# Cross-attention on one core: copied rows of reciprocals, transfers over all partitions, and another order on ACT and in the first unit

## The chip, the cores and the metric

The kernel runs on one core of one Trainium2 chip. The metric is the device time of one execution in microseconds (us). The kernel before was run three times: 1737.68, 1738.79 and 1740.34 us, median 1738.79 us.

## The reference

Sixteen batches of 1024 queries (x, 512 wide) attend to 64 context rows each, with 16 heads of 64. The residual is added, and the sum goes through a layer norm:

```
qh = x @ Wq + bq;  kh = ctx @ Wk + bk;  vh = ctx @ Wv + bv
attn = exp(qh.kh * mask - max(over everything)) * mask
attn = attn / (sum over keys + 1e-15)
y = (attn @ vh) @ Wo + bo + x
out = (y - mean) / sqrt(var + 1e-5) * gamma + beta
```

The maximum is one number over all batches and heads, so no exponential can be taken before every score is known.

## The kernel before

The program has two phases. **scores_phase** (to about 905 us of the span) computes all masked scores. Heads go in pairs: a tile has 128 partitions (two heads of 64 keys) and 512 queries, and a unit is 8 such pairs for 512 queries. There are 32 units. The scores of units 0 and 1 stay in SBUF (`s32`), those of the other 30 go to DRAM. The products of the value weights and Wo (`u`) go to DRAM too.

**output_phase** is where the diff lies. Its loops run over 8 groups of 4 units. For each unit:

- SP loads the scores (2 MB, `load_scores`), the residual x (1 MB, `load_x`), for every second unit u (2 MB, `load_u`), and stores y (1 MB, `store_y`, L774), which waits until POOL has finished the unit.
- ACT takes the exponentials of the scores in place in two halves of 1.9 us (`exps`, L884). `tiny` (L892) fills the bank of sums first.
- PE sums them over the keys of each head with 16 small matmuls (`sums`, L832), into 32 rows of each of four quarters. DVE inverts the sums (`invert`, L966).
- SP writes the reciprocals to DRAM (`store_r`, L743: 4 transfers of 8 rows) and reads them back over the partitions (`spread_r`, L751: 4 transfers, each one 8 KB row to 64 partitions, 512 KB), since each of the 64 key rows of a head needs the same reciprocals. Between them SP waits for the stores to land (L754).
- DVE multiplies the exponentials by the reciprocals (`scale_p`, L973), ACT rounds the product to f16 (`round_p`, L898), DVE takes the rest (`split_p`, L983). Eight pairs, three PSUM banks in turn.
- PE multiplies both halves by u for four tiles of 128 queries (`unit`, L846: 96 matmuls), and behind the fourth pair of the third tile come the sums of the unit three further on. Four output banks, which ACT fills with the bias beforehand (`fill`, L904).
- DVE adds the residual and takes mean and variance (`residual`, L988: L997, L1000, L1002), POOL makes 1/std and the shift (`inv_std`, L1063), ACT normalizes (`norm`, L909), POOL multiplies by gamma and adds beta (`affine`, L1076: L1080, L1082).

Every engine takes its instructions in a fixed order written out by hand. Within the turn of unit n PE multiplies unit n, DVE and ACT make the halves of unit n+1 (p 0 to 7), ACT takes the exponentials and PE the sums of unit n+3. DVE's order (L1004) is: scale 0, 1, split 0, scale 2, split 1, residual 0, scale 3, split 2, scale 4, split 3, residual 1, scale 5, split 4, scale 6, split 5, scale 7, split 6, invert, residual 2, split 7, residual 3. ACT's order before (L914) is halves 0 and 1, tiny, first half of the exponentials, halves 2 and 3, fill 0, norm 0, second half, halves 4 and 5, fill 1, norm 1, halves 6 and 7, fill 2, norm 2, fill 3, norm 3. POOL alternates `inv_std` and `affine` for the tiles 0 to 3. SP's order (L796) is store_y of the last unit, load_scores of the unit four on, load_x, load_u, store_r and spread_r of the unit three on.

At the start of the phase SP issues loads of scores 2 and 3, u, the three rows gamma, beta and bo over 128 partitions, and x 0 and 1. PE's first five matmuls, which only write the banks once, wait for u (L870), and ACT's first instruction waits for them (L941).

Of the kernel before, what the change touches and what calls it, by code (L numbers as in the profile page):

```python
# [5 lines left out]
F32 = mybir.dt.float32  # L6
# [26 lines left out]
SBANKS, GBANKS, OBANKS, RBANKS = 2, 4, 4, 3  # L33
EARLY = NP // 2
# [8 lines left out]
def build(nc, xT, x, ctxT, maskT, wk, wqT, wv, wo, bk, bq, bv, bo, gamma, beta,  # L43
# [4 lines left out]
    r_d = nc.dram_tensor("reciprocals", (UNITS, 2, NP, TT), F32, kind="Internal").ap()  # L48
# [621 lines left out]
def output_phase(nc, x, scores_d, u_d, r_d, bo, gamma, beta, sel_sum_d, out,  # L670
# [4 lines left out]
    with ExitStack() as ctx:  # L675
# [59 lines left out]
        def _(sp):  # L735
# [7 lines left out]
            def store_r(n, u):  # L743

                sp.wait_ge(r_done, n + 1)
                for q in range(4):
                    th, a = q // 2, q % 2
                    sp.dma_start(r_d[u % UNITS, :, 4 * a:4 * a + 4, th * HT:(th + 1) * HT],
                                 r32[32 * q:32 * q + NP, u % 2, :]).then_inc(r_stored, 16)

            def spread_r(n, u):  # L751


                sp.wait_ge(r_stored, 64 * n + 64)  # L754
# [29 lines left out]
            load_scores(3, 3)  # L784
# [44 lines left out]
        def _(pe):  # L829
# [44 lines left out]
            pe.wait_ge(sum_in, 16)  # L874
# [7 lines left out]
        def _(act):  # L882
# [31 lines left out]
            def group(g, last):  # L914
                for u in range(UNITS):
                    n, s = g * UNITS + u, (u + 1) % 2
                    more, more3 = not (last and u == UNITS - 1), not (last and u >= UNITS - 3)
                    halves = lambda *ps: [round_p(n + 1, s, p) for p in ps] if more else None
                    halves(0, 1)
                    if more3:  # L920
                        tiny(n + 3)
                        exps(n + 3, u + 3, 0)
                    halves(2, 3)
                    if more:
                        fill(n + 1, 0)
                    norm(g, u, 0)
# [12 lines left out]
                    norm(g, u, 3)  # L939
# [10 lines left out]
            for t in range(TB):  # L950
                fill(0, t)
# [5 lines left out]
            with act.Fori(0, NG - 1) as g:  # L957
                group(g, False)
            group(NG - 1, True)

        @block.vector
        def _(dve):
# [3 lines left out]
            def invert(n, u):  # L966

                dve.wait_ge(e_summed, n + 1)
                if not (isinstance(n, int) and n < 2):
                    dve.wait_ge(r_stored, 64 * (n - 1))  # L970
                dve.reciprocal(r32[:, u % 2, :], ps_sum[:, 0:HT]).then_inc(r_done, 1)  # L971

            def scale_p(n, u, p):  # L973
                s = u % 2
                if p % 4 == 0:
                    dve.wait_ge(bc_in[s][p // 4], 16 * n - 16 * s + 32)
# [159 lines left out]
```

## Time and profile before

| | before |
|---|---|
| median of three runs | 1738.79 us |
| the profiled execution | 1738.39 us |
| its span | 1736.5 us |
| mean granted TensorE clock | 0.982 |
| PE, DVE, ACT, POOL busy | 93%, 66%, 54%, 31% |
| output phase, from / to | about 905 / 1736.5 us |

The busy shares are means over both phases. POOL works only in the second, so its 544.1 us are two thirds of that phase. Times below are counted from the start of the span. A row of the timeline gives start, length, engine, line, what is written and read, count, and in brackets how long the engine had been idle and what ended that.

### The profile page before, as it was taken

The page shows a single profiled execution, that of the slowest core. Times are in us where ns is not written, and L with a number is a line of the kernel's source. Part 1 is how long each engine was busy: PE and PEld are TensorE (multiplying, and loading weights), DVE is VectorE, ACT ScalarE, POOL GpSimd, SP SyncE. Part 2 cuts the span into 40 slices and gives each one's busy share as a digit, 9 for nine tenths or more (in the row PEclk, how much of TensorE's full clock was granted, in tenths as well). Part 3 has the DMA queues.
Part 4 walks back from the last instruction along what each step waited for, and adds up shares of the span by engine and source line. Part 5 has one row for each costly group of instructions (what it writes and reads, how often), then busy time and mean ns, then how long its engine had stood idle before and what let it go on. Part 6 is the DMA issues. An engine that isn't in the chain of part 4 may idle for free. (4 is left out here: it accounts for less than half of the span.)

```text
span 1736.5 us, 30465 instructions
## 1 busy us (share of the span) xinstructions
PE 1619.3 (93%) x10501; PEld 796.7 (46%) x10501; DVE 1151.8 (66%) x2138; ACT 935.5 (54%) x1383; POOL 544.1 (31%) x778
## 2 busy tenths in 40 slices
PE   4999999999999999999983999999999999999997
PEld 4445555455554555545531344444444444444443
DVE  6666555565556655566542777878778787878774
ACT  6755555555555555555534555555555555555542
POOL 0000000000000000000000567677666767677677
PEclk8999999999999999999995999999999999999999
DMA  6463444534445444453327999999999999999971
GB/s 231 146 226 121 164 176 151 222 122 160 172 157 217 127 154 172 163 211 128 153 97 247 265 308 314 290 286 292 313 318 295 291 313 316 278 293 297 310 234 73
DMA packets 92556, 382.11 MB, mean 220 GB/s; under 512 B 7520, under 2 KB 12768, under 8 KB 74592
## 3 DMA queue, kind: packets, MB, share of 16 engines
q1 hardware_dynamic: 92512, 381.53, 65.7%
q8 instruction: 27, 0.44, 0.1%
q14 instruction: 17, 0.14, 0.0%
HBM read 250.43 MB, written 131.07 MB: 220 GB/s over the span
## 5 line engine op out<-in xcount | busy, mean ns | idle before, releaser
L78 PE MATMUL ps_o<-u,p_hi 128*128 128x512 f16 x1024 | 389.7, 381 | 5.0 <-DVE p_lo L985 5.0
L69 PE MATMUL ps_s<-x_hi,g_hi 128*128 128x512 f16 x1024 | 389.1, 380 | 3.7 <-ACT s L496 3.7
L79 PE MATMUL ps_o<-u,p_hi 128*128 128x512 f16 x1024 | 389.4, 380 | 0.0
L80 PE MATMUL ps_o<-u,p_lo 128*128 128x512 f16 x1024 | 389.2, 380 | 0.0
L71 PE MATMUL ps_s<-x_hi,g_lo 128*128 128x512 f16 x1024 | 388.8, 380 | 0.0
L70 PE MATMUL ps_s<-x_lo,g_hi 128*128 128x512 f16 x1024 | 388.6, 380 | 0.0
L496 ACT ACTIVATE s<-ps_s,c_bias 128x512 f32<-128x512 f32 x256 | 176.1, 688 | 314.1 <-PE ps_s L71 311.0
L1052 POOL MEMSET zeros<- 128x256 f32 x1 | 0.3, 311 | 905.9 <-POOLq L138 905.9
L985 DVE TENSOR_TENSOR p_lo<-ps_p,p_hi 128x512 f16<-128x512 f32 x256 | 175.4, 685 | 126.3 <-ACT p_hi L902 126.0
L616 DVE TENSOR_TENSOR score_max<-score_max,tile_max 128x1 f32<-128x1 f32 x257 | 40.7, 158 | 310.5 <-ACT s L496 308.8
L912 ACT ACTIVATE y<-y,shift,rstd 128x512 f32<-128x512 f32 x128 | 104.1, 813 | 243.4 <-POOL shift L1073 238.9
L1080 POOL TENSOR_TENSOR y<-y,gamma_b 128x512 f32<-128x512 f32 x128 | 163.4, 1277 | 118.4 <-ACT y L912 118.4
L1082 POOL TENSOR_TENSOR y<-y,beta_b 128x512 f32<-128x512 f32 x128 | 191.9, 1499 | 10.0
L626 DVE CUSTOM_DVE_ANT_0 s<-s,mask_add 128x512 f32<-128x512 f32 x256 | 176.4, 689 | 0.3 <-issue 0.3
L902 ACT ACTIVATE p_hi<-ps_p 128x512 f16<-128x512 f32 x256 | 140.7, 584 | 49.7 <-DVE ps_p L980 49.7
L78 PEld LDWEIGHTS ps_o<-u,p_hi 128*128 128x128 f16 x1024 | 100.3, 98 | 138.5 <-issue 12.8
L69 PEld LDWEIGHTS ps_s<-x_hi,g_hi 128*128 128x128 f16 x1024 | 100.2, 98 | 127.1 <-issue 10.8
L80 PEld LDWEIGHTS ps_o<-u,p_lo 128*128 128x128 f16 x1024 | 100.5, 98 | 121.6 <-issue 1.5
L71 PEld LDWEIGHTS ps_s<-x_hi,g_lo 128*128 128x128 f16 x1024 | 100.3, 98 | 121.3 <-issue 0.8
L79 PEld LDWEIGHTS ps_o<-u,p_hi 128*128 128x128 f16 x1024 | 100.5, 98 | 116.8 <-issue 0.6
L70 PEld LDWEIGHTS ps_s<-x_lo,g_hi 128*128 128x128 f16 x1024 | 100.3, 98 | 112.8 <-issue 0.8
L980 DVE TENSOR_TENSOR ps_p<-s_more,r_bc 128x512 f32<-128x512 f32 x128 | 116.5, 921 | 5.4 <-DMA r_bc<-reciprocals 4.1
(90 smaller groups left out, 2363.1 us busy)
## 6 DMA issues: line engine op xcount, KB each, us to landing
r_bc<-reciprocals SPq DMA_DIRECT2D x128, 512.0 KB, 8.1
scores<-s SPq DMA_DIRECT2D x30, 2048.0 KB, 7.6
x<-xT_in SPq DMA_DIRECT2D x32, 1024.0 KB, 9.5
u_halves<-u_out SPq DMA_DIRECT2D x64, 512.0 KB, 3.2
s_more<-scores SPq DMA_DIRECT2D x16, 2048.0 KB, 16.3
u<-u_halves SPq DMA_DIRECT2D x16, 2048.0 KB, 22.3
y<-x_in SPq DMA_DIRECT2D x32, 1024.0 KB, 18.1
out<-y SPq DMA_DIRECT2D x31, 1024.0 KB, 12.3
```

The costliest lines, as they stand in the source:

```text
L69: pe.matmul(out, lhs_hi, rhs_hi, start=first, stop=False)
L70: pe.matmul(out, lhs_hi, rhs_lo, start=False, stop=False)
L71: return pe.matmul(out, lhs_lo, rhs_hi, start=False, stop=last)
L78: pe.matmul(out, lhs_hi, rhs_hi, start=False, stop=False, skip_group_check=True)
L79: pe.matmul(out, lhs_hi, rhs_lo, start=False, stop=False, skip_group_check=True)
L80: return pe.matmul(out, lhs_lo, rhs_hi, start=False, stop=False, skip_group_check=True)
L496: act.activation(s32[:, u % 2, p, :], ps_s[p % SBANKS][:, :], ACT.Identity, bias=c_bias[:, k:k + 1], scale=1 / (G_SCALE * X_SCALE)).then_i ...
L626: dve.tensor_tensor_reduce(s32[:, u % 2, p, :], s32[:, u % 2, p, :], mask_add[:, j, t0:t0 + TT], 1.0, MASKED, ALU.add, ALU.max, tile_max[: ...
L902: act.activation(p_hi[:, s, p, :], ps_p[p % RBANKS][:, :], ACT.Copy).then_inc(p_hi_done, 1)
L985: dve.tensor_tensor(p_lo[:, s, p, :], ps_p[p % RBANKS][:, :], p_hi[:, s, p, :], ALU.subtract)\
L1080: pool.tensor_tensor(y, y, gamma_b[:, :], ALU.mult).then_inc(scaled, 1)
L1082: pool.tensor_tensor(y, y, beta_b[:, :], ALU.add).then_inc(shifted, 1)
```

## The change

It has four parts.

1. **Copies.** The selection matrix gives each sum not once but four times, in 16 rows per head (16 h + p + 4 j); the matmuls keep their shape. `store_r` writes these rows twice, so that DRAM holds eight copies: 16 transfers of 16 rows of 1 KB (256 KB) instead of 4 of 8 rows. `spread_r` is 2 transfers instead of 4, each over all 128 partitions (1 MB); 16 source rows of 8 KB (2 heads x 8 copies), each read by 8 partitions.
2. **ACT's order.** In a unit: tiny, half 0, fill 3 of this unit, half 1, exponentials' first half, norm 2 of the unit before, half 2, exponentials' second half, half 3, norm 3 of the unit before, fill 0, halves 4 and 5, norm 0, fill 1, halves 6 and 7, norm 1, fill 2. Norms 2 and 3 are thus taken in the next unit's turn. The first group is taken out of the loop.
3. **Start of the phase on SP.** Scores 3 and x 1 are loaded only behind the first store_r and spread_r.
4. **First matmuls.** The five matmuls that write the banks take the selection matrix (64 KB) and scores already in SBUF (f32) instead of u, and wait for that load alone.

```diff
-    r_d = nc.dram_tensor("reciprocals", (UNITS, 2, NP, TT), F32, kind="Internal").ap()
+    r_d = nc.dram_tensor("reciprocals", (UNITS, 2, 2, COPIES, NP // 2, TT), F32, kind="Internal").ap()
...
                 for q in range(4):
                     th, a = q // 2, q % 2
-                    sp.dma_start(r_d[u % UNITS, :, 4 * a:4 * a + 4, th * HT:(th + 1) * HT],
-                                 r32[32 * q:32 * q + NP, u % 2, :]).then_inc(r_stored, 16)
+                    for c in range(0, COPIES, 4):
+                        for h in range(2):
+                            rows = 32 * q + 16 * h
+                            sp.dma_start(r_d[u % UNITS, a, h, c:c + 4, :, th * HT:(th + 1) * HT]
+                                         .rearrange("c p t -> (c p) t"),
+                                         r32[rows:rows + 16, u % 2, :]).then_inc(r_stored, 16)
...
                 for k in range(2):
-                    for h in range(2):
-                        rows = r_d[u % UNITS, h:h + 1, 4 * k:4 * k + 4, :].rearrange("a p t -> a (p t)")
-                        sp.dma_start(r_bc[rows_of(h), u % 2, 4 * k:4 * k + 4, :].rearrange("r p t -> r (p t)"),
-                                     rows.to_broadcast([NK, 4 * TT])).then_inc(bc_in[u % 2][k], 16)
+                    rows = r_d[u % UNITS, k, :, :, :, :].rearrange("h c p t -> (h c) (p t)").unsqueeze(1)
+                    sp.dma_start(r_bc[:, u % 2, 4 * k:4 * k + 4, :].rearrange("r p t -> r (p t)"),
+                                 rows.to_broadcast([2 * COPIES, P // (2 * COPIES), 4 * TT])).then_inc(bc_in[u % 2][k], 16)
...
             load_scores(2, 2)
-            load_scores(3, 3)
             load_u(0, B - 1)
...
             load_x(0, 0)
+            store_r(0, 0)
+            spread_r(0, 0)
+            load_scores(3, 3)
             load_x(0, 1)
-            for n in range(2):
-                store_r(n, n)
-                spread_r(n, n)
+            store_r(1, 1)
+            spread_r(1, 1)
             store_r(2, 2)
...
-            pe.wait_ge(u_in[0], 16)
-            for o in (*ps_o, ps_sum):
-                mm = pe.matmul(o[:, :], u2[:, 0, 0, 0, 0:P], u2[:, 0, 0, 0, :], start=True, stop=True)
+            pe.wait_ge(sum_in, 16)
+            for o in (ps_sum, *ps_o):
+                mm = pe.matmul(o[:, :], sel_sum[:, :, :].rearrange("r a b -> r (a b)"), scores_of(0)[:, 0, :],
+                               start=True, stop=True)
...
-                    halves(0, 1)
+                    behind = lambda t: None if first and u == 0 else norm(g if u else g - 1, (u - 1) % UNITS, t)
                     if more3:
                         tiny(n + 3)
+                    halves(0)
+                    fill(n, 3)
+                    halves(1)
+                    if more3:
                         exps(n + 3, u + 3, 0)
-                    halves(2, 3)
+                    behind(2)
+                    halves(2)
+                    if more3:
+                        exps(n + 3, u + 3, 1)
+                    halves(3)
+                    behind(3)
                     if more:
                         fill(n + 1, 0)
+                    halves(4, 5)
                     norm(g, u, 0)
-                    if more3:
-                        exps(n + 3, u + 3, 1)
-                    halves(4, 5)
                     if more:
                         fill(n + 1, 1)
+                    halves(6, 7)
                     norm(g, u, 1)
-                    halves(6, 7)
                     if more:
                         fill(n + 1, 2)
-                    norm(g, u, 2)
-                    if more:
-                        fill(n + 1, 3)
-                    norm(g, u, 3)
...
-            sel_sum[h * NK:(h + 1) * NK, p % 4, 4 * h + p % 4] = 1.0 / P_SCALE
+            sel_sum[h * NK:(h + 1) * NK, p % 4, 16 * h + p % 4:16 * h + 16:4] = 1.0 / P_SCALE
```

## Rows read from the trace of the kernel before

**Rows 1.** The page: shares of the engines in the chain that ended last.

```profile
POOL 21%; DVE 10%; issue 6%; ACT 5%; DMA 3%; SPq 1%; DVEq 1%; ACTq 0%; PE 0%; POOLq 0%
```

**Rows 2.** Waits from 1200 to 1400: total us, times, longest.

```profile
ACT y L912 <- POOL shift L1073: 62.4, 25, 4.1
...
PE ps_sum L841 <- ACT s_more L890: 5.9, 4, 1.5
```

**Rows 3.** Timeline of PE, the sums of units 2, 3 and 28.

```profile
1017.71 2.11 PE L841 MATMUL ps_sum<-s,sel_sum 128*32 128x256 f32 x32
1040.58 1.07 PE L841 MATMUL ps_sum<-s_more,sel_sum 128*32 128x256 f32 x16
...
1649.84 1.07 PE L841 MATMUL ps_sum<-s_more,sel_sum 128*32 128x256 f32 x16
1652.77 1.07 PE L841 MATMUL ps_sum<-s_more,sel_sum 128*32 128x256 f32 x16 [1.86 <-ACT s_more L890]
```

**Rows 4.** Timelines of POOL, DVE and ACT within one unit.

```profile
1321.57 1.27 POOL L1080 TENSOR_TENSOR y<-y,gamma_b 128x512 f32<-128x512 f32 x1 [0.93 <-ACT y L912]
1322.91 1.60 POOL L1082 TENSOR_TENSOR y<-y,beta_b 128x512 f32<-128x512 f32 x1
...
1321.88 3.19 DVE L980 TENSOR_TENSOR ps_p<-s,r_bc 128x512 f32<-128x512 f32 x2
...
1326.05 0.81 ACT L912 ACTIVATE y<-y,shift,rstd 128x512 f32<-128x512 f32 x1 [4.08 <-POOL shift L1073]
```

**Rows 5.** Groups of the output phase by form: busy us, mean ns, idle before.

```profile
L985 DVE TENSOR_TENSOR p_lo<-ps_p,p_hi 128x512 f16<-128x512 f32 x256 | 175.4, 685 | 126.3 <-ACT p_hi L902 126.0
...
L902 ACT ACTIVATE p_hi<-ps_p 128x512 f16<-128x512 f32 x256 | 140.7, 584 | 49.7 <-DVE ps_p L980 49.7
...
L1000 DVE BATCH_NORM_STATS2 stats<-y 128x6 f32<-128x512 f32 x128 | 88.9, 694 | 4.4
L997 DVE SCALAR_TENSOR_TENSOR y<-ps_o,y 128x512 f32<-128x512 f32 x128 | 85.8, 670 | 15.0 <-PE ps_o L80 12.4
...
L971 DVE RECIPROCAL r<-ps_sum 128x256 f32<-128x256 f32 x32 | 56.0, 1749 | 28.2 <-PE ps_sum L841 28.2
```

**Rows 6.** Stretches: length, busy us (count) of PE, PEld, DVE, ACT, POOL, clock, DMA share, GB/s.

```profile
910.00:922.00 12.00, 0.00 (x0) 0.00 (x0) 0.15 (x1) 0.00 (x0) 0.48 (x4) 0.50 1.01 430
925.00:927.00 2.00, 2.00 (x5) 0.46 (x3) 0.00 (x0) 0.00 (x0) 0.00 (x0) 0.50 1.01 194
...
942.00:948.00 6.00, 3.74 (x32) 1.28 (x32) 1.40 (x1) 2.54 (x2) 0.00 (x0) 0.58 1.01 218
```

**Rows 7.** Start of the output phase: timelines of PE, ACT, DVE and SP.

```profile
924.74 1.89 PE L872 MATMUL ps_o<-u 128*128 128x512 f16 x4 [20.45 <-DMA u<-u_halves]
...
927.50 7.66 ACT L890 ACTIVATE s<-s,neg_max 128x2048 f32<-128x2048 f32 x4
...
914.77 0.15 DVE L1038 TENSOR_SCALAR neg_max<-key_max 128x1 f32<-128x1 f32 x1 [7.89 <-POOL key_max L1055]
...
948.27 1.27 DVE L980 TENSOR_TENSOR ps_p<-s,r_bc 128x512 f32<-128x512 f32 x2
...
935.23 2.62 SPq L748 DMA_DIRECT2D reciprocals<-r  x4
939.02 2.41 SPq L760 DMA_DIRECT2D r_bc<-reciprocals  x4
```

**Rows 8.** Issues of spreads (ns min/median/max), and of loads (KB, us to landing).

```profile
L760 SPq DMA_DIRECT2D r_bc<-reciprocals x128: 496/592/1382, 939.0 to 1670.6; - x128
...
s_more<-scores SPq DMA_DIRECT2D x16, 2048.0 KB, 16.3
```

**Rows 9.** Last unit: timelines of POOL and DVE.

```profile
1706.39 0.19 POOL L1066 TENSOR_TENSOR var_eps<-mean_var,ln_eps 128x1 f32<-128x1 f32 x1 [0.17 <-DVE mean_var L1002]
...
1732.70 1.26 POOL L1082 TENSOR_TENSOR y<-y,beta_b 128x512 f32<-128x512 f32 x1
...
1723.98 0.69 DVE L997 SCALAR_TENSOR_TENSOR y<-ps_o,y 128x512 f32<-128x512 f32 x1 [3.51 <-PE ps_o L80]
```

More of the change, by code:

```diff
@@ L33 @@
 SBANKS, GBANKS, OBANKS, RBANKS = 2, 4, 4, 3
+COPIES = 8
+STORES_R = 2 * COPIES
 EARLY = NP // 2
@@ L747, in store_r @@
                     th, a = q // 2, q % 2
-                    sp.dma_start(r_d[u % UNITS, :, 4 * a:4 * a + 4, th * HT:(th + 1) * HT],
-                                 r32[32 * q:32 * q + NP, u % 2, :]).then_inc(r_stored, 16)
+                    for c in range(0, COPIES, 4):
[4 more added lines that the diff above has]
+                                         r32[rows:rows + 16, u % 2, :]).then_inc(r_stored, 16)
             def spread_r(n, u):
-                sp.wait_ge(r_stored, 64 * n + 64)
+                sp.wait_ge(r_stored, 16 * STORES_R * (n + 1))
                 if isinstance(n, int) and n == 2:
@@ L867, in group @@
                     unit(g, u, last)
-            pe.wait_ge(u_in[0], 16)
-            for o in (*ps_o, ps_sum):
-                mm = pe.matmul(o[:, :], u2[:, 0, 0, 0, 0:P], u2[:, 0, 0, 0, :], start=True, stop=True)
+            pe.wait_ge(sum_in, 16)
+            for o in (ps_sum, *ps_o):
+                mm = pe.matmul(o[:, :], sel_sum[:, :, :].rearrange("r a b -> r (a b)"), scores_of(0)[:, 0, :],
+                               start=True, stop=True)
             mm.then_inc(o_written, 1)
-            pe.wait_ge(sum_in, 16)
             for n in range(3):
@@ L912, in norm, with group @@
                 act.activation(y, y, ACT.Identity, bias=shift[:, t:t + 1], scale=rstd[:, t:t + 1]).then_inc(normed, 1)
-            def group(g, last):
+            def group(g, first, last):
                 for u in range(UNITS):
@@ L918, in group @@
                     halves = lambda *ps: [round_p(n + 1, s, p) for p in ps] if more else None
-                    halves(0, 1)
+                    behind = lambda t: None if first and u == 0 else norm(g if u else g - 1, (u - 1) % UNITS, t)
                     if more3:
                         tiny(n + 3)
+                    halves(0)
+                    fill(n, 3)
+                    halves(1)
+                    if more3:
                         exps(n + 3, u + 3, 0)
-                    halves(2, 3)
+                    behind(2)
[4 more added lines that the diff above has]
+                    behind(3)
                     if more:
                         fill(n + 1, 0)
+                    halves(4, 5)
                     norm(g, u, 0)
-                    if more3:
-                        exps(n + 3, u + 3, 1)
-                    halves(4, 5)
                     if more:
                         fill(n + 1, 1)
+                    halves(6, 7)
                     norm(g, u, 1)
-                    halves(6, 7)
                     if more:
                         fill(n + 1, 2)
-                    norm(g, u, 2)
-                    if more:
-                        fill(n + 1, 3)
-                    norm(g, u, 3)
+                if last:
+                    norm(g, UNITS - 1, 2)
+                    norm(g, UNITS - 1, 3)
             act.wait_ge(o_written, 1)
@@ L949, in _ @@
             act.wait_ge(affine_in, 48)
-            for t in range(TB):
+            for t in range(TB - 1):
                 fill(0, t)
@@ L956, in _ @@
                 round_p(0, 0, p)
-            with act.Fori(0, NG - 1) as g:
-                group(g, False)
-            group(NG - 1, True)
+            group(0, True, False)
+            with act.Fori(1, NG - 1) as g:
+                group(g, False, False)
+            group(NG - 1, False, True)
         @block.vector
@@ L969, in invert @@
                 if not (isinstance(n, int) and n < 2):
-                    dve.wait_ge(r_stored, 64 * (n - 1))
+                    dve.wait_ge(r_stored, 16 * STORES_R * (n - 1))
                 dve.reciprocal(r32[:, u % 2, :], ps_sum[:, 0:HT]).then_inc(r_done, 1)
@@ L975, in scale_p @@
                 if p % 4 == 0:
-                    dve.wait_ge(bc_in[s][p // 4], 16 * n - 16 * s + 32)
+                    dve.wait_ge(bc_in[s][p // 4], 8 * n - 8 * s + 16)
                 if p >= RBANKS or not (isinstance(n, int) and n == 0):
```

## The prediction

> **What bounds the kernel now.** I read the page first. PE is the busiest engine by far, yet the chain that ended last has POOL with 21%, DVE with 10% and PE with 0% [rows 1]. So somewhere PE waits for a ring of the others. The waits of a stretch in the middle say where: in each unit PE waits 1.5 us for the exponentials (5.9 us in four waits on one buffer, and the same again on the other), while ACT itself has waited up to 4.1 us for POOL's shift [rows 2]. The exponentials are late because they stand in ACT's order behind norms and halves that wait.
>
> What this costs is read from the starts of the sums. Unit 3 has them at 1040.58 and unit 28 at 1649.84, so 25 periods of 24.37 us. Unit 2 has both halves of its sums in one piece of 2.11 us and is followed by unit 3 after 22.87 us [rows 3]. So 22.87 us is a unit in which PE doesn't wait, and 24.37 us one with its wait of 1.5. PE can give at most 1.50 us per unit.
>
> The start of the phase is bound otherwise. PE waits 20.45 us for u, and only then can the first exponential begin, at 927.50, although the negated maximum is there at 914.77 + 0.15 [rows 7].
>
> **Start of the phase.** The selection matrix is 64 KB and the first transfer that the phase issues; I estimate its landing at 908.5, some 3 us into the phase, as the 8 KB stores need 3.8 us from the first of four issues to all landed [rows 7]. Five f32 matmuls with 512 columns follow. The nearest row is the pair of sum blocks of unit 2: 32 records, 2.11 us, four groups of 256 columns one after the other, 0.53 each [rows 3], so 1.06 for 512 columns at 2.4 GHz and 2.1 at 1.2 GHz. The granted clock was 0.50 from 910 on, after PE had stood still [rows 6]. Both ends: 908.5 + 5.3 = 914, and 908.5 + 10.5 = 919. I take 917.5, since PE begins again before the level fell. With the filling of the sums' bank the exponentials start at 918 instead of 927.5: 9.5 us earlier (12 at most).
>
> From there to the first scaling it was 20.8 us (948.27 - 927.50), and DVE got there through three inversions. Now the stores are 16 instead of 4. Four took 2.62 us, 0.64 each, and the first spread was issued 3.8 us after the first store [rows 7]. Sixteen take 10.2 and land 1.2 later. First reciprocals at 918 + 7.7 = 925.7, landed at 937, first spread (1 MB) at 430 GB/s 2.5 us plus 1.5: scaling starts at 941, gain 7.3 us. The longer chain of stores eats 2 of the 9.5.
>
> Unit 1's reciprocals then stand behind 3 MB of loads (7.4 us) and 16 more stores, so that they are there at about 955, where the sums of unit 3 are due at 959: PE waits some 1.5 us. Unit 2's come behind 5 MB (12.5 us), at about 979, and cost PE about 1.5 more. Before, these two units cost more: from the first scaling at 948.27 to the start of unit 2 (its sums at 1017.71, less 20 of the 32 steps of a unit's 22.87 - 2.11 = 20.76 us ahead of them, so 1004.7) were 56.4 us. Mine are 941 to 995. **Start: 9.7 us.**
>
> **The transfers.** While only spreads were in flight the DMA moved 218 GB/s at full share, and 430 while it was loads [rows 6]. A unit's 2.1 MB of reciprocals so take 9.7 us, and its 5.2 MB of loads and stores 12.2; that is 22 of 24.4 us. Which property of the spreads costs the half? Two are candidates: 64 partitions per transfer, and one source row read by all. The gamma, beta and bo loads read one row too, go to all partitions, and moved 194 GB/s [rows 6]. The new transfer changes both: 128 partitions, and 16 rows. I take 430 GB/s, thus 4.9 us, and keep 9.7 as the other end.
>
> The Trainium skill's page "SBUF — State Buffer" (The DMA port swizzle) says that a transfer to partitions 0 to 63 reaches eight of sixteen ports, about 218 GB/s, and one to all partitions up to 436. By it alone the copies would be needless; the load of one row at 194 GB/s speaks against its being the whole story, and both readings give 4.9 us here.
>
> Stores: 16 issues at 0.64 are 10.2 us of SP's time instead of 2.6; spreads 2 at 0.6 are 1.2 instead of 2.4. SP's turn grows by 6.4 us per unit. The bounds for one are the shortest and the longest issue of a spread, 0.5 and 1.38 [rows 8]; I take 0.64, from the stores themselves.
>
> **ACT's order: the new ring.** Start from norm 0. Lengths are those of [rows 4, 5, 7], less 0.1 where two follow on one engine (four exponentials took 7.66, so 1.9 each); a fill is taken as long as a half, both being one ACT pass over 128x512. Norm 0, fill 1, half 6: 0.7 + 0.5 + 0.6 = 1.8. DVE: split 6 0.6, inversion 1.7, residual 2 1.6 (0.67 + 0.69 and the aggregate), split 7 0.6, residual 3 1.6, scale 0 0.7 = 6.8. ACT: half 0 0.5, fill 3 0.5, half 1 0.5, exponentials 1.9 = 3.4. Then norm 2 to POOL 0.9, affine 2 1.27 + 1.60 = 2.9, inv_std 3 1.55 (from 1324.51 to norm 3 at 1326.05), norm 3 0.9, affine 3 2.9, inv_std 0 1.7 = 10.9. **The ring is 22.9 to 23.0 us**, just at PE's 22.87. Inside it the second half of the exponentials ends 3.1 us after norm 2 starts, ahead of PE's need, so the wait of 1.5 goes. What is late next is DVE's scale 0: it is behind residual 3, and that behind everything.
>
> Cover that thins: norm 2 now waits for the exponentials, so store_y, and load_scores behind it on SP, come some 4 us later in a unit, and the scores are wanted some 5 us earlier. From affine 3's end to the next use are 11.5 us; the landing took 16.3 in the middle [rows 8]. But that queue held 9.7 us of spreads. In order: stores end, land, spread issued, 4.9 us of spreads, 1 MB out and 2 MB scores 7.4 us, 1.5 to land. With SP's stores from the inversion on (15 us after norm 2), and a period P, the load lands at 15.05 - P + 10.2 + 1.9 + 4.9 + 7.4 + 1.5 = 41 - P after norm 2, and must be there at P - 1.9: satisfied for P above 21.4. No wait at 23.0, with 3 us to spare. PE's instructions, the number and size of the matmuls of the sums, POOL's and DVE's work are the same.
>
> 25 periods x (24.37 - 23.0) = 34.3 us, and unit 28, whose period had 0.4 us more wait (1.86), 1.8.
>
> **The end.** POOL's last run goes from 1706.39 to 1733.96 without a pause, while PE ends at 1723.9 [rows 9]. By the new order POOL enters the last three units up to 5.7 us later, and there PE's unit (20.8 us, no sums) is no longer than POOL's round (four times 0.9 + 2.9 + 1.55, so 21.4), so this isn't caught up: I count 5 us lost, between 0 and 5.7.
>
> **Sum:** 9.7 + 34.3 + 1.8 - 5.0 = 40.8 us of the profiled execution's 1738.39, so 1697.6; against the median of 1738.79, 0.4 above it, 1698.0. The scores phase is untouched.
>
> **Rivals.**
>
> *The ring is longer* (22%). Scale 0 falls beside POOL's affine 1. Two scales beside affine 2 took 3.19 us [rows 4], two undisturbed 1.27 [rows 7]. One such delay of 0.8 in the ring gives P = 23.8: 25 x 0.57 = 14 us, so 1718; half of it 1708. For: it is a matter of a few tenths. Against: affine 1 is nearly over by then. The page "SBUF — State Buffer" calls the port pair that DVE and GpSimd share an exclusive lock, held for a whole instruction; by it scale 0 would wait for the whole of a 1.27 or 1.60 us instruction, and the sum would be the 1718 of this case.
>
> *Spreads stay at 218 GB/s* (7%): 9.7 in place of 4.9 gives 2P = 45.8 + 1.9, P = 23.9; the start gains 4 less. About 1724.
>
> *Only the start gains* (5%): something else holds the period at 24.37 and the end loses its 5: 1734.
>
> *SP becomes the bound* (8%): this one is slower. SP waits in turn for stores, spreads, then store_y and the scores. With i us per store the formula is 2P = 32.7 + 16 i; at 0.64 P = 21.5 doesn't bind, it equals the old 24.37 at i = 1.0, and the whole is slower than before from 1.05 on, since the longer stores eat the start's gain too and the end loses its 5. At 1.38 P is 27.4 and the time 1738.8 + 25 x 3.0 = about 1814; at 1.1, 25.1 and 1757. For: stores with 16 rows are a form not yet seen, behind a full queue. Against: the four took 2.62, and the new ones are as short.
>
> *The change doesn't do it at all* (3%): the five f32 matmuls or the fetch of a first group outside the loop eat the start, the ring stays: within 0.2%.
>
> **How the numbers follow.** My forecast has 55%, with its own range 1686 to 1706 (P from 22.87 to 23.2, start 7 to 12, end 0 to 5.7). With the longer ring it reaches 1720, and with slow spreads 1727. 1686 to 1727 holds some 82%. A difference under 0.2% (3.5 us) can't be told from none here. Faster by more: 55 + 22 + 7 + 5 = 89, less a little for their tails, 88%; same 4%; slower 8%.
>
> **What would show it.** Right: PE's waits on L890 vanish from the middle and the sums of two units lie 22.9 to 23.1 apart; stretches with spreads alone show above 400 GB/s; the first exponential starts between 915 and 919; 16 stores take about 10 us; POOL never waits for DVE's mean but for ACT's norm 2. Wrong: PE still waits there; ACT's exponentials wait for s or s_more from the DMA; SP's queue shows store_y or load_scores waiting behind the stores; scale 0 at 1.5 us each time.

## The result, and the profile after

The changed kernel is slower: 1829.43 us, median of four runs (1828.32 to 1832.28), against 1738.66 for the kernel before (1737.68 to 1740.34). The ratio is 1.0523, 95% interval 1.0505 to 1.0542. The forecast was 1698.

I take the loss apart by the starts of the sums, as in [rows 3]. PE of the changed kernel:

```profile
1042.17 2.08 PE L848 MATMUL ps_sum<-s_more,sel_sum 128*32 128x256 f32 x32
...
1735.13 1.93 PE L848 MATMUL ps_sum<-s_more,sel_sum 128*32 128x256 f32 x16 [5.05 <-ACT s_more L897]
```

Unit 3 has its sums at 1042.17 and unit 28 at 1735.13. The period is therefore 27.72 us where it was 24.37. That is 25 x 3.35 = 83.7 us. The start is 1.6 later than before, and from unit 28's sums to the end of the span it is 91.0 instead of 86.7, so 4.3 more. Together 89.6, the difference of the spans (1826.1 and 1736.5). The mean granted clock fell from 0.982 to 0.951 along with PE's waits; in e8 and e15 below, where PE hardly waits, it is 0.985. ("Unit 3" and "unit 28" are here, as in [rows 3], the turns in which PE multiplies these units; the sums in them belong to the unit three further on.)

The page's chain that ended last, engines and then lines (before: [rows 1]):

```profile
DMA 24%; POOL 9%; SPq 6%; ACT 4%; issue 4%; DVE 2%; PE 0%; ACTq 0%; DVEq 0%; POOLq 0%
DMA reciprocals<-r 8%; DMA s<-scores 7%; DMA s_more<-scores 7%; SPq L753 5%; POOL y L1096 3%; POOL y L1094 3%; ACT y L919 2%; DVE r L985 1%; POOL rstd L1084 1%; DMA r_bc<-reciprocals 1%; SPq L766 1%; POOL var_eps L1080 1%; POOL shift L1087 1%; ACT p_hi L909 1%; ACT s L897 1%
```

POOL and DVE led it before with 31% together; now DMA and SP's queue have 30%, most of it by the landings of the stores (8%) and of the scores (7% and 7%). The waits from 1200 to 1400 (total, times, longest; before: [rows 2]), of the engines:

```profile
POOL y L1094 <- ACT y L919: 73.3, 28, 11.3
...
ACT s L897 <- DMA s<-scores: 20.3, 4, 7.3
...
PE ps_sum L848 <- ACT s L897: 13.5, 6, 4.6
ACT s_more L897 <- DMA s_more<-scores: 11.2, 3, 7.0
```

And of SP in the same stretch:

```profile
SPq L766 <- DMA reciprocals<-r: 78.3, 7, 12.1
SPq L753 <- DVE r L985: 22.8, 7, 3.5
SPq L783 <- POOL y L1096: 11.0, 3, 4.1
```

PE waits for the exponentials, they wait up to 7.3 us for the scores' landing, and SP stands 11 us per unit in the wait for the stores. Its timeline has the whole ring:

```profile
1306.33 7.32 SPq L753 DMA_DIRECT2D reciprocals<-r  x16
1325.62 1.20 SPq L766 DMA_DIRECT2D r_bc<-reciprocals  x2
1327.09 0.41 SPq L783 DMA_DIRECT2D out<-y  x1
1327.76 0.37 SPq L741 DMA_DIRECT2D s<-scores  x1
1328.32 0.38 SPq L773 DMA_DIRECT2D y<-x_in  x1
1331.97 8.03 SPq L753 DMA_DIRECT2D reciprocals<-r  x16
1350.64 1.19 SPq L766 DMA_DIRECT2D r_bc<-reciprocals  x2
...
1362.02 7.35 SPq L753 DMA_DIRECT2D reciprocals<-r  x16
```

Sixteen stores are issued from 1306.33 to 1313.65 and seen landed at 1325.62, 12.0 us after the last. Only then go out the spreads and the scores' load (1327.76). Those scores land at 1345.31, when ACT begins their exponentials after 7.29 us of idling; their stores begin at 1362.02. The round from store to store is 55.7 us for two units, or 27.8 for one. The granted clock falls behind PE's wait, to 0.50 from 1349 to 1353. This doesn't visibly lengthen the round: from the waited-for exponentials to the next stores it is 16.7 us here and 16.7 in e1 below (1349.43 to 1366.14), where the clock was 0.78 or more in each stretch of 4 us. Meanwhile the queue (length, busy us of the engines, clock, DMA share, GB/s; before: [rows 6]):

```profile
1300.00:1306.00 6.00, 6.00 (x29) 2.72 (x28) 4.08 (x5) 2.30 (x4) 4.87 (x10) 1.00 1.01 218
1306.00:1312.00 6.00, 6.00 (x29) 2.74 (x28) 5.70 (x11) 2.91 (x6) 4.84 (x8) 1.00 1.04 391
...
1323.50:1327.00 3.50, 3.50 (x18) 1.57 (x17) 3.50 (x5) 0.98 (x2) 3.42 (x5) 1.00 0.02 7
```

The spreads still move 218 GB/s, as before. The bulk loads follow, the stores land only behind them, and then for 3.5 us hardly anything is in flight (share 0.02), until the next spread begins.

The same ring was there in the kernel before, where it did not bind yet. Its timeline of SP:

```profile
1317.96 2.55 SPq L748 DMA_DIRECT2D reciprocals<-r  x4
1330.27 2.41 SPq L760 DMA_DIRECT2D r_bc<-reciprocals  x4
```

And its waits of SP from 1200 to 1400:

```profile
SPq L760 <- DMA reciprocals<-r: 68.6, 8, 9.9
```

Four stores took 12.3 us from their first issue to the next spread; sixteen now 19.3. With 9.7 of spreads, 12.2 of bulk and about 2.2 idle, I estimate that the old queue needed 24.1 of the 24.37 us. The estimate is a little low: where this ring binds with the same stores and spreads (e1 and e3 below), the period is 24.56 and 24.66. That it didn't bind before is seen in the starts of the sums, which lie 24.36 to 24.38 us apart in every unit from 3 to 28. In e1 they lie 22.69 to 26.55 apart, and in the changed kernel up to 29.4.

### The profile page after: what moved, and what is told of

Same layout as the page of the kernel before. It is cut to its first block and busy times, and to the rows that moved or that the text cites. A ratio compares the mean times of both kernels' runs of the same rounds, so it can differ in the third digit from the quotient of the medians.

```text
span 1826.1 us, 30718 instructions
## 1 busy us (share of the span) xinstructions
PE 1667.3 (91%) x10506; PEld 807.6 (44%) x10506; DVE 1147.0 (63%) x2138; ACT 936.1 (51%) x1383; POOL 515.9 (28%) x778
## 5 line engine op out<-in xcount | busy, mean ns | idle before, releaser
L80 PE MATMUL ps_o<-u,p_hi 128*128 128x512 f16 x1024 | 399.2, 390 | 9.5 <-DVE p_lo L999 9.3
L81 PE MATMUL ps_o<-u,p_hi 128*128 128x512 f16 x1024 | 397.6, 388 | 0.0
L82 PE MATMUL ps_o<-u,p_lo 128*128 128x512 f16 x1024 | 397.0, 388 | 0.0
L909 ACT ACTIVATE p_hi<-ps_p 128x512 f16<-128x512 f32 x256 | 146.4, 585 | 140.2 <-DVE ps_p L994 140.2
L1096 POOL TENSOR_TENSOR y<-y,beta_b 128x512 f32<-128x512 f32 x128 | 182.4, 1425 | 10.0
L82 PEld LDWEIGHTS ps_o<-u,p_lo 128*128 128x128 f16 x1024 | 102.1, 100 | 127.7 <-issue 12.3
L994 DVE TENSOR_TENSOR ps_p<-s,r_bc 128x512 f32<-128x512 f32 x128 | 110.8, 877 | 16.5 <-DMA r_bc<-reciprocals 13.5
```

The lines of the kernel that those rows point to most:

```text
L80: pe.matmul(out, lhs_hi, rhs_hi, start=False, stop=False, skip_group_check=True)
L81: pe.matmul(out, lhs_hi, rhs_lo, start=False, stop=False, skip_group_check=True)
L82: return pe.matmul(out, lhs_lo, rhs_hi, start=False, stop=False, skip_group_check=True)
L909: act.activation(p_hi[:, s, p, :], ps_p[p % RBANKS][:, :], ACT.Copy).then_inc(p_hi_done, 1)
L1096: pool.tensor_tensor(y, y, beta_b[:, :], ALU.add).then_inc(shifted, 1)
```

## The experiments

Periods below are those of units 3 to 28, from the starts of the sums. **Theory A:** the ring through SP's order and its one queue binds; it is as long as spreads, bulk, and the time that the stores and SP leave the queue idle. **Rivals:** the new ACT order or the new start costs it; or one cause alone (the spreads' form, the stores' bytes). e5, e7, e11 and e13 were run once each.

### Which part of the change

e1 is the changed kernel with part 1 taken back, e2 is before with part 1 alone, e3 with part 2 alone, e4 with parts 3 and 4 alone. The parts stand in the diff of the change; the core of e1, against the changed kernel:

```diff
-                            sp.dma_start(r_d[u % UNITS, a, h, c:c + 4, :, th * HT:(th + 1) * HT]
-                                         .rearrange("c p t -> (c p) t"),
-                                         r32[rows:rows + 16, u % 2, :]).then_inc(r_stored, 16)
+                    sp.dma_start(r_d[u % UNITS, :, 4 * a:4 * a + 4, th * HT:(th + 1) * HT],
+                                 r32[32 * q:32 * q + NP, u % 2, :]).then_inc(r_stored, 16)
...
-                                 rows.to_broadcast([2 * COPIES, P // (2 * COPIES), 4 * TT])).then_inc(bc_in[u % 2][k], 16)
+                                     rows.to_broadcast([NK, 4 * TT])).then_inc(bc_in[u % 2][k], 16)
```

> The changed kernel with its first part undone: stores of 4 transfers and spreads of 4 half-partition transfers as before; ACT's order and the start stay changed. Theory A (the ring is SP's and the DMA's: spreads, bulk behind them, stores landing behind the bulk, and the 16 stores made it longer): the ring is that of before, about 9.7 + 12.2 + 2.2 = 24.1 us a unit, so the period returns to 24.1 to 24.5 and with the start's gain the time is 1725 to 1735. Theory B (the new order of ACT wants the scores too early, and the loads are late whatever the stores are): ACT still waits several us for scores in many units, period above 25.5, time above 1770.

> The kernel before with the first part alone: 16 stores of copied rows and 2 spreads over all partitions. Theory A: the ring through SP and the DMA is as in the changed kernel, 27 to 28 us a unit where the scores or the reciprocals come late, time 1800 to 1835. Theory B (ACT's order is needed for the loss): ACT takes the exponentials later here, so the loads are in time, and the time is within 1738 to 1760.

> The kernel before with ACT's new order alone. Theory A: the DMA ring of about 24.1 to 24.4 us binds in place of the engines' ring of 24.37, so nearly nothing changes: 1730 to 1742, PE's wait of 1.5 us becomes a wait of ACT for scores from the DMA. Theory B: loads too late, period above 25.5, time above 1770. The forecast of step one (the engines' ring alone) would give 1738.8 - 34 + 5 = 1703 to 1712.

> The kernel before with the third and fourth part alone: order of SP's first transfers, and first matmuls that wait for the selection matrix. All theories: the first exponential starts at 915 to 919 instead of 927.5 and the gain is 5 to 12 us: 1727 to 1734. If the start isn't what ends the phase (the DMA's queue is as full as before, only in another order), the gain is under 3 us: above 1736.

| | us | ratio to before, 95% | period |
|---|---|---|---|
| e1 | 1740.27 | 1.0011 (1.0001 to 1.0021) | 24.56 |
| e2 | 1827.02 | 1.0517 (1.0500 to 1.0535) | 27.51 |
| e3 | 1743.65 | 1.0030 (1.0019 to 1.0042) | 24.66 |
| e4 | 1733.41 | 0.9970 (0.9959 to 0.9981) | 24.36 |

The copies alone are the whole loss. ACT's order by itself costs 5 us, though its ring is shorter (e8 below), and the start by itself gains 5. In e1 the ring through SP and the queue binds. The waits from 1200 to 1400 show it, ACT's for the scores:

```profile
ACT s L893 <- DMA s<-scores: 9.1, 3, 3.1
```

and SP's for the stores:

```profile
SPq L762 <- DMA reciprocals<-r: 74.5, 8, 9.9
SPq L779 <- POOL y L1092: 31.9, 8, 5.8
```

The second row is part of the ring too: store_y stands ahead of the scores' load in SP's order, and waits for POOL. Whether the scores' load ahead of store_y would help was not tried.

### Why the spread stays slow

In e5, e6, e7 and e11 the spreads of the kernel before read rows of x instead of the reciprocals: 64 different rows to each half of the partitions (e5), 128 different rows in one transfer (e6), 16 blocks of 8 different rows, the changed kernel's form (e7), and one row for all 128 (e11). The diff has the row that goes, then e6's and e7's.

```diff
-                        rows = r_d[u % UNITS, h:h + 1, 4 * k:4 * k + 4, :].rearrange("a p t -> a (p t)")
+                    rows = x.rearrange("b (r q) d -> (b r) (q d)", q=4)[128 * k:128 * k + P, :]
...
+                    rows = x.rearrange("b (c r q) d -> (b c) r (q d)", q=4, r=16)[16 * k:16 * k + 16, 0:8, :]
```

> The kernel before, whose spreads keep their form (4 transfers to 64 partitions) but read 64 different 8 KB rows of x instead of one row 64 times; the reciprocals are thus not used. What halves the rate of the spreads? If it is the 64 partitions: about 218 GB/s while only spreads are in flight. If it is the repeated row: about 430 GB/s.

> The kernel before with spreads as 2 transfers of 128 different 8 KB rows of x to 128 partitions (reciprocals not used). Both readings of the rate: 430 GB/s, unless 8 KB rows are slow in themselves. For the time: if before was bound by the ring of ACT, DVE and POOL alone, as I read it, the period stays at 24.37 and the time within 1733 to 1741; if the DMA's ring was what held it, it falls by 1 us a unit or more, below 1715.

> As the run with 128 different rows, but described as 16 blocks of 8 rows, the blocks not adjacent in DRAM, as the changed kernel's spread is described (16 source rows, each for 8 partitions). If the changed kernel's 213 GB/s comes from reading each row eight times: 430 GB/s here. If it comes from how 16 blocks of 8 neighbouring partitions are dealt to the engines: about 215 GB/s here.

> Before with the spreads as two transfers, each of ONE row of 8 KB read for all 128 partitions (a row of x; the reciprocals are not used, the output is not the reference's). Asks whether reading one row many times is slow by itself. If only the way the partitions are dealt out costs (the form of 16 blocks of 8, and 64 partitions): spreads alone at 380 to 460 GB/s, as e6 with 128 different rows. If repeated reading costs as well: 190 to 230 GB/s, near the 194 of the gamma, beta and bo loads. The time is then 1735 to 1742 either way, since the engines' ring of 24.4 us stays.

A stretch with spreads alone in e5 (columns as above):

```profile
1311.00:1317.00 6.00, 4.54 (x45) 1.93 (x38) 4.70 (x9) 4.34 (x6) 4.74 (x6) 1.00 1.01 218
```

in e6:

```profile
1324.00:1327.00 3.00, 3.00 (x16) 1.37 (x14) 1.56 (x3) 2.89 (x5) 2.00 (x3) 1.00 1.01 423
```

and in e11:

```profile
1325.00:1328.00 3.00, 3.00 (x15) 1.37 (x14) 1.36 (x3) 2.69 (x5) 1.92 (x4) 1.00 0.99 401
```

e7, in one of the microseconds with its spreads alone:

```profile
1309.00:1310.00 1.00, 1.00 (x9) 0.35 (x10) 1.00 (x2) 0.86 (x2) 0.49 (x2) 1.00 1.08 238
```

Over the whole of them e7 moved 188 to 287 GB/s, mostly 238. So reading one row of 8 KB many times is not slow, and different rows do not help: what counts is the way the transfer is laid over the partitions. The times moved little (1741.63, 1739.54 and 1737.69 us for e5, e7 and e11; 1736.24 for e6, ratio 0.9986, 0.9977 to 0.9996), because ACT's ring is still there: in e6 too the sums lie 24.33 to 24.39 us apart.

e13 measures ten layouts one after the other, each waited for, in the quiet queue ahead of the phase.

```diff
+            for i, m in enumerate((1, 2, 4, 8, 16, 32, 64)):
+                of = rows[0:m, :].unsqueeze(1).to_broadcast([m, P // m, 4 * TT]) if m > 1 else rows[0:1, :].to_broadcast([P, 4 * TT])
+                sp.dma_start(to, of).then_inc(form_in[i + 1], 16)
+                sp.wait_ge(form_in[i + 1], 16)
```

> Before, with a row of transfers ahead of the last phase's first load, one at a time, each waited for, into the buffer of the reciprocals (overwritten later; the whole result is computed). In this order: 1 MB to all 128 partitions from 128 rows; from 1 row read by all; from 2, 4, 8, 16, 32 and 64 rows, each read by a block of 64, 32, 16, 8, 4 and 2 neighbouring partitions; then 512 KB to partitions 0 to 63 from one row; then both halves so, two transfers together as in the kernel before. Theory (the way the rows are dealt out decides, and a block form with 16 blocks of neighbours is the bad one): 128 rows and 1 row near 430 GB/s, so 2.4 us and a latency of about 2; 16 blocks near 210, 4.9 us and the latency; 32 and 64 blocks like 16; of 2, 4 and 8 blocks I do not know, 430 or 215. The one to 64 partitions: 2.4 us for half the bytes, and the pair about 5. Rival (every read of a row by neighbours in blocks is slow): all of 2 to 64 near 215. The whole becomes 40 to 70 us longer, which counts for nothing.

A stretch out of each (the lines of length, busy times, clock, share, GB/s again): 128 rows, 1 row, then 2, 4, 8, 16, 32 and 64 blocks, 64 partitions, and the pair as in the kernel before.

```profile
909.00:911.00 2.00, 0.00 (x0) 0.00 (x0) 0.00 (x0) 0.00 (x0) 0.00 (x0) 0.50 0.98 418
914.00:915.00 1.00, 0.00 (x0) 0.00 (x0) 0.00 (x0) 0.00 (x0) 0.32 (x4) 0.50 1.12 467
920.00:937.00 17.00, 0.00 (x0) 0.00 (x0) 0.00 (x0) 0.00 (x0) 0.00 (x0) 0.50 0.12 53
941.00:954.00 13.00, 0.00 (x0) 0.00 (x0) 0.00 (x0) 0.00 (x0) 0.00 (x0) 0.50 0.25 71
960.00:966.00 6.00, 0.00 (x0) 0.00 (x0) 0.00 (x0) 0.00 (x0) 0.00 (x0) 0.50 0.52 116
970.00:973.00 3.00, 0.00 (x0) 0.00 (x0) 0.00 (x0) 0.00 (x0) 0.00 (x0) 0.50 1.00 221
977.00:978.00 1.00, 0.00 (x0) 0.00 (x0) 0.00 (x0) 0.00 (x0) 0.00 (x0) 0.50 1.05 426
982.00:983.00 1.00, 0.00 (x0) 0.00 (x0) 0.00 (x0) 0.00 (x0) 0.00 (x0) 0.50 1.07 442
986.00:987.00 1.00, 0.00 (x0) 0.00 (x0) 0.00 (x0) 0.00 (x0) 0.00 (x0) 0.50 1.13 328
991.00:994.00 3.00, 0.00 (x0) 0.00 (x0) 0.00 (x0) 0.00 (x0) 0.00 (x0) 0.50 1.08 232
```

Two columns count. With 2, 4 and 8 blocks the DMA share is 0.12, 0.25 and 0.52: 2, 4 and 8 of 16 DMA engines work. With 16 blocks of 8 all of them are busy and move half. The two faults overlap: GB/s by the engines at work are about 27 each with 2 blocks, 18 with 4, 14 with 8 and with 16, and 26 to 29 in the fast forms. With 32 blocks of 4, 64 of 2, one row or 128 rows they move 418 to 467. The pair to 64 partitions each moves 232; the 328 of a single transfer to 64 is one microsecond out of three (131, 328 and 66 GB/s, shares 0.69, 1.13 and 0.33), which together come to some 244 at full share. (My guess that 32 and 64 blocks would be like 16 was wrong, and that 2, 4 and 8 keep engines idle I had not thought of.)

The Trainium skill's page "DMA: Bandwidth & Descriptors" (Why a DMA increments its semaphore by 16 and not by 1) says that the slowest dimension sets the number of engines that a transfer uses; the shares agree. Its section "The descriptor swizzle" gives each engine groups of 4 neighbouring partitions in a transfer to 128; that 16 blocks of 8 break this order and the finer ones keep it is my reading of it, and no run here shows which engine wrote where. Why 16 blocks of 8 are slow stays open; that they are is measured.

### What the stores cost

e10 is e2 with the same 256 KB of stores in two transfers of 128 rows, and e7's rows of x. e8 is e1 with e6's spreads, e12 the changed kernel with them. In all three the reciprocals are stored but not used.

```diff
-                for q in range(4):
...
+                for c in range(2):
+                    sp.dma_start(r_d[u % UNITS, c].rearrange("h c p (e t) -> (h c p e) t", t=HT),
+                                 r32[:, u % 2, :]).then_inc(r_stored, 16)
```

> ACT's new order and the new start, with the 4 old stores and with fast spreads (128 different rows of x, reciprocals not used). This takes the DMA's ring down to about 4.9 + 12.2 + 2.2 = 19.3 us. Forecast's ring (22.9 to 23.2 us a unit by ACT, DVE and POOL): 1695 to 1708, no wait of ACT for scores. If the new order's ring of engines is longer than I worked out (23.8): about 1718. If the loads are late for another reason than the spreads: above 1725.

> Base is e2 (before with the changed stores and spreads alone). The 256 KB of the stores go out as two transfers of 128 rows instead of sixteen of 16 rows, and the spreads read rows of x in the same form and size instead of the reciprocals, so the reciprocals are not used and the output is not the reference's. If the number of small transfers costs (their issue, 7.3 us of SP, and the tail until the last is counted): near 1740 us, with SP's issue of the stores below 1.5 us. If it is the 256 KB in place of 64 KB, or where the stores stand in the order: near e2's 1827.

> The changed kernel whole, with its sixteen stores, but its two spreads read 128 different rows of x, the form that moved 385 to 467 GB/s in e6; the reciprocals are stored but not used, so the output is not the reference's. Theory A: the DMA ring is 4.9 (spreads) + 12.2 (bulk) + 5 to 6 (stores' tail, SP, issue) = 22 to 23, about the engines' ring: 1692 to 1712 us; so the loss is the product of slow spreads and many stores, and either alone would be bearable. Rival (sixteen stores cost by themselves, by SP's 7.3 us of issuing and the landing): the time stays above 1725.

e10 took 1758.61 us (1.0114, 1.0100 to 1.0129). With the same slow form of spreads, four stores gave 1739.54 (e7, one run) and sixteen 1827.02 (e2). Of the 87 us some 68 go with the sixteen transfers in place of two; e2 also spreads the copies and e10 rows of x, so this is not the number alone. The 19 left are what e10 has more than e7, where the bytes are the likely cause, not a shown one.

e8 took 1691.92 us (0.9733, 0.9717 to 0.9750), period 23.10, and of the waits for the scores' landing 0.2 us are left in its middle. This is the forecast ring, once the queue is out of the way. e12, with sixteen stores, took 1737.67 (0.9993, 0.9983 to 1.0003), period 24.51. I had expected 1692 to 1712, so sixteen stores do cost by themselves, 46 us where the spreads move 430 GB/s, and 89 where they move 218 (e1 to the changed kernel). This is what e12's rival said. The ring of theory A stands, but my 5 to 6 us for the stores' tail were too few.

### The order on SP, and versions that win

e9 is e1 with the stores issued ahead of the loads of x and u, so that less stands before them in the queue and x and u fill the time until SP sees them landed.

```diff
                     if not last:
                         load_scores(n + UNITS, u)
+                    if not (last and u >= UNITS - 3):
+                        if first and u == 0:
+                            spread_r(2, 2)
+                        store_r(n + 3, u + 3)
...
-                        if first and u == 0:
-                            spread_r(2, 2)
-                        store_r(n + 3, u + 3)
                         spread_r(n + 3, u + 3)
```

> The whole result is computed. Base is e1 (changed exponentials' order and start, the old four stores and four spreads); in SP's order the four stores of the reciprocals now stand directly behind store_y and the scores' load, and the loads of x and u come behind the stores, ahead of the next spreads. Theory A (the ring that binds is SP's order with the DMA queue: stores land only behind the bulk ahead of them, and the queue is idle for about 4 us from their landing to the next spread): the stores now have less bulk ahead, and x and u fill the time until SP sees them landed, so the DMA's ring falls from 24.1 to about 22 and the engines' ring of 22.9 to 23.3 binds: 1695 to 1710 us, ACT no longer waits for the scores' landing. Rival (the order of the loads does not matter, it is the bytes at their rate): as e1, 1737 to 1743.

> The whole result is computed. The changed kernel with its sixteen stores and 16 blocks of 8 partitions, only SP's order altered as in e9 and e15: the stores ahead of the loads of x and u. Theory A (a ring through SP and its queue, whose length is the waiting of the stores behind the bulk plus the slow spreads): the ring loses up to a transfer time of x and u (3 MB in two units, some 5 us at most per unit) but keeps 9.7 us of spreads and 7.3 us of issuing: period 24.5 to 26, so 1740 to 1780 us, between e9's 1726 and the changed kernel's 1829. Rival (the order matters only in e15, through its stores of 512 KB): above 1815.

e9 took 1726.31 (1719.04 to 1728.96; 0.9929, 0.9917 to 0.9942), a third to a half of the fall that I expected. Its period of 23.87 is from the trace of the fastest run, so at the median it is up to 0.3 longer. The order does what it was meant to do: from the last store's issue to the next spread it is 4.2 us on average (1200 to 1500) where it was 9.6 in e1. e16, the changed kernel with this order, took 1783.94 (1.0267, 1.0250 to 1.0285), period 25.94: with the stores ahead 45 of the 91 us come back. The same distance is 5.0 us where it was 11.2.

e14 has real reciprocals in a fast form: sixteen copies, so 32 blocks of 4, written by four stores of all 128 rows (512 KB). DVE reads the halves of the tokens from two places.

```diff
+                for e in range(STORES_R):
+                    sp.dma_start(r_d[u % UNITS, :, :, :, e, :, :, :].rearrange("x a h c p t -> (x a h) (c p t)"),
+                                 r32[:, u % 2, :]).then_inc(r_stored, 16)
...
+                    for e in range(2):
+                        rows = r_d[u % UNITS, e, k, :, :, :, :, :].rearrange("h e c p t -> (h e c) (p t)").unsqueeze(1)
+                        sp.dma_start(r_bc[:, u % 2, 4 * k + 2 * e:4 * k + 2 * e + 2, :].rearrange("r p t -> r (p t)"),
+                                     rows.to_broadcast([2 * COPIES, P // (2 * COPIES), 2 * TT])).then_inc(bc_in[u % 2][k], 16)
```

> The whole result is computed. The changed kernel with sixteen copies instead of eight, so that a row is read by blocks of 4 neighbouring partitions (32 blocks, the form that moved 344 to 426 GB/s one by one in e13), and with four stores of all 128 partitions (128 KB each) instead of sixteen of 16. The reciprocals' layout has the two halves of the tokens apart, so the spreads are four transfers of 512 KB to all partitions. Theory (the loss comes from the form of 16 blocks of 8 at 218 GB/s together with the small stores): spreads alone at 340 GB/s and over, the DMA's ring 4.9 to 6 + 12.2 + about 1.5 for 512 KB of stores + some 3 = about 22, so the engines' ring of 22.9 to 23.3 binds: 1692 to 1712 us. Rival (real copies in DRAM, written and read back, cost more than rows of x did in e8, or the bytes of the stores do): 1720 or above, and ACT waits for the scores' landing.

> The whole result is computed. e14 and in SP's order the stores ahead of the loads of x and u, as in e9. If e14 is at the engines' ring (1692 to 1712): the same within 6 us. If in e14 the DMA's ring still binds, this one is below it by up to 15 us (e9 was 14 us below e1).

e14 took 1746.73 us (1.0052, 1.0039 to 1.0066), period 24.85: the rival. Behind the bulk its stores run at half the share; the stretch before the next spread:

```profile
1329.50:1334.00 4.50, 4.50 (x45) 2.00 (x44) 3.19 (x7) 2.96 (x6) 3.50 (x6) 1.00 0.48 178
1334.00:1335.00 1.00, 1.00 (x6) 0.49 (x5) 1.00 (x3) 0.22 (x1) 0.92 (x2) 1.00 0.00 0
```

Their outermost dimension is 8 blocks, and as with the 8 blocks of e13 (0.52) half of the engines carry them, and at the tail of the queue nothing else runs. In **e15**, with the order of e9, they stand ahead of x and u, which fill the rest. It took **1700.17 us (1699.06 to 1701.52), ratio 0.9781, 0.9768 to 0.9795**: it beats both kernels, with the whole result computed. Its sums of units 3 and 28:

```profile
1028.86 1.93 PE L845 MATMUL ps_sum<-s_more,sel_sum 128*32 128x256 f32 x32
...
1608.36 1.93 PE L845 MATMUL ps_sum<-s_more,sel_sum 128*32 128x256 f32 x32
```

A stretch with its spreads in flight:

```profile
1305.00:1308.00 3.00, 3.00 (x36) 1.46 (x38) 2.27 (x4) 2.43 (x3) 2.92 (x4) 1.00 1.09 465
```

SP's waits from 1200 to 1400:

```profile
SPq L779 <- POOL y L1096: 54.1, 8, 7.4
SPq L749 <- DVE r L982: 40.4, 9, 4.6
SPq L762 <- DMA reciprocals<-r: 37.5, 9, 5.4
```

The period is 23.18, close to e8's, and ACT no longer waits for the scores. SP now waits longest for POOL, and 4 us instead of 11 for the stores.

The periods side by side (us; "order": stores ahead of x and u; ACT's new order in all):

| | 4 small stores | 16 small stores | 4 stores of 128 KB |
|---|---|---|---|
| spreads at 218 GB/s | 24.56 (e1) | 27.72 (changed) | |
| the same, order | 23.87 (e9) | 25.94 (e16) | |
| spreads near 430 GB/s | 23.10 (e8) | 24.51 (e12) | 24.85 (e14) |
| the same, order | | | 23.18 (e15) |

Where the queue binds, sixteen small stores add 3.2 us to a period (27.72 - 24.56), and slow spreads 3.2 (27.72 - 24.51). If the two simply add, the queue without either would need about 21.3, hidden beneath the engines' 23.1. That last number is worked out, not measured.

## Why the prediction was wrong

**What bounds the kernel.** I named one ring, that of ACT, DVE and POOL, and it was there. I did not see how close a second one stood to its 24.37. The chain's 0% for PE says only that PE isn't the bound, and the waits I listed were those of the engines, not SP's. SP's row (68.6 us in 8 waits for the stores' landing) has what my sum needed: 8.6 us on average, not 1.9. It doesn't say by itself that the ring binds: in e8, where it doesn't, the row has 73.3 us in 9 waits. I had also worked out that the queue is busy for 22 of 24.4 us, and read that as room.

**The step that failed** is "Stores: 16 issues at 0.64 ... stores end, land", with 1.9 us for the landing. It came from the start of the phase [rows 7], where the queue was nearly empty (from the end of the fourth issue it is 1.2 there, as the sum of the start has it). In the middle the stores land behind all the bulk issued ahead of them: 9.8 us after the last of four issues, 12.0 after the last of sixteen. With 12.0 in place of 1.9, and 9.7 of spreads in place of 4.9, my 41 - P becomes 55.9 - P, less 2.9 for the quicker issues (7.3 instead of 10.2), so 53.0 - P. To be at most P - 1.9 it wants P = 27.4; 27.72 was measured. So two terms were of another stretch or another form. The formula itself is only half borne out. With their own terms it gives 23.8 for e1 (2.5 of issues, 9.6 to the landing, 9.7 of spreads) and 23.0 for e12 (7.4, 7.9, 4.9), where 24.56 and 24.51 were measured. What it leaves out is SP's wait for POOL ahead of the scores' load: 31.9 us in e1, 20.3 in e12 and only 11.0 in the changed kernel, each in 200 us. That this closes the gap is not shown.

**The spreads** were the second failed term: taken at 430 GB/s because the form changed in two properties, measured at 218. I had priced this as a rival (P 23.9, 1724 us) but with the stores' landing at 1.9 beside it. It was right that 64 partitions are one cause; the new form brought another. The other candidate, one row read by all, I took from the 194 GB/s of gamma, beta and bo [rows 6]. With a row of 8 KB, e11 and e13 show 401 to 467. Why the three rows of 2 KB were slow stays open.

**SP as the bound** was the rival that came closest, and for the wrong reason. Its point of decision was 1.05 us per issue. An issue took 0.46 (7.3 for sixteen), less than my 0.64. What cost was landing, not issuing.

**ACT's order** was nearly right: 22.9 to 23.0 forecast, 23.10 measured in e8, 23.18 in e15. e8's first eight units take 22.69 each and the later ones 23.2 on average. So the ring is nearer 23.2, and PE's own unit is 22.69, not 22.87. PE's waits on the exponentials are gone in both runs. The ring was not stretched to 23.8 by scale 0.

**Start.** The first exponential was forecast between 915 and 919 and came at 914.44; the first scaling at 938.04 instead of 941. Yet the gain at unit 3's sums, which I took as 9.7, is -1.6 in the changed kernel, 4.5 in e4 (1036.11 against 1040.58), 8.3 in e1, 11.7 in e15 and 17.9 in e8: units 1 and 2 stand behind the same stores. In the changed kernel unit 1's first scaling waited 11.4 us for its reciprocals, until 959.94, where I had 955.

**End.** 5 us lost were forecast, 2.4 are measured in e8 and e15 (89.0 from unit 28's sums instead of 86.7), 4.3 in the changed kernel. My reading of [rows 9] was wrong: POOL does pause there, 0.93 us ahead of each first multiplication, and its tiles start 4.6 us apart (1708.41, 1713.01), so its round is 18.4 us and not 21.4. That is below PE's 20.8, so part of the delay can be caught up.

In e8 the terms are 31.9 (period), 17.9 (start) and -2.4, together 47.4 us off the span. My 40.8 had the gain of the periods too large (34.3 + 1.8) and that of the start too small (9.7); that the sum comes near is partly luck. e8 has the old stores and unused reciprocals, so it shows the engines' part of the forecast, not the change.

## What to carry to other kernels

When one queue carries small transfers that somebody waits for among bulk loads, take their landing from the middle of the trace, and follow the issuing engine's order as a ring: issue, landing behind the bulk, next issue. Its wait alone doesn't tell whether the ring binds (68.6 us before, 73.3 in e8); the engines' waits for what it loads, and uneven periods, do. Count the ring in each period even where it is hidden, since one that is just shorter than the bound makes a gain elsewhere worth nothing (e1, e3). Issue the small, waited-for stores ahead of loads that are not urgent, and look at the DMA share beside the GB/s, since a share of 0.12 and a share of 1.0 at half the rate are different faults.

## What the runs showed that I had not expected

- A transfer to all 128 partitions is not fast for that alone: from 16 blocks of 8 neighbours it moved 221 GB/s with all DMA engines busy, from 32 blocks of 4 it moved 426, and from 2 blocks 53, by two engines.
- One 8 KB row read by 128 partitions moved 401 to 467 GB/s; so many readers of such a row cost nothing here.
- The stores of 256 KB, some 3% of the unit's 7.6 MB, cost 89 us as sixteen transfers behind the bulk where the spreads move 218 GB/s, and 46 where they move 430.
- The order of the same issues on SP was worth 14, 45 and 47 us (e9, e16, e15 against e1, the changed kernel and e14).
